# Group-norm sums from ScalarE's accumulator, and the order of ScalarE's, GpSimd's and TensorE's work around them

## The chip, the cores and the metric

One core of a Trainium2 chip. The metric is the device time of one execution in microseconds; below, "the median" is that of three runs. The engines are TensorE (PE, its weight loads PEld), VectorE (DVE), ScalarE (ACT), GpSimd (POOL) and SyncE (SP), which here issues the DMAs. A name with q (POOLq) is the engine's sequencer.

## What is computed

Eight batches of 548 tokens (36 image patches, embedded, and 512 text tokens) with 192 features pass one attention layer with three heads of 64, decay in place of a mask and a group norm over each head's outputs, and one FFN of 16 experts with a top-8 router. Cut to what matters here:

```
h = concat(image @ W.T + b, txt)                        # (8, 548, 192)
q, k, v = layernorm(h) @ Wq.T, ... @ Wk.T, ... @ Wv.T   # 3 heads of 64
weights = softmax(q @ k.T / 8 * decay)                  # per head
o = weights @ v
mean, var = o.mean(axis=(tokens, 64)), o.var(axis=(tokens, 64))   # per batch and head
y = (o - mean) / sqrt(var + 1e-5) * gn_weight + gn_bias
h = h + y @ Wo.T
x2 = layernorm(h)
h = h + sum over experts e of comb[:, e] * (gelu(x2 @ w1[:, e]) @ w2[e, :])
```

## The kernel before

All products are made in split precision: an operand is rounded to fp32r (hi), the rest is kept (lo), and PE adds hi x hi, lo x hi and hi x lo. ACT rounds (a Copy that writes hi), DVE subtracts (lo); POOL does both for w1 and w2.

**Attention** is a loop over the batches, written out by hand for each engine; `body(b, ...)` of an engine is its part of batch b together with what is left of batch t = b - 1. PE's order in it: q and k of batch b in three products of ten matmuls (`qk`, the third gives head 3's q in rows 0 to 63 and its k in rows 64 to 127), the transposes of the third head's weights of batch t (`probs_transpose(t, 2)`), the scores of heads 1 and 2 (`scores_pair`), `attend(t, 2)`, head 3's scores (`scores_third`), v (`values`), the output product of batch b - 2 (`project`), then transposes and `attend` for heads 1 and 2 of b, the transposes of the next batch's tokens (`x_transpose`) and the group-norm sums of t (`gn_sums`). A full first pass of qk needs xa and xb, which ACT rounds (`x_hi`) and DVE subtracts (`x_lo`), after DVE's sum over tokens (`x_ext`).

ACT's order in `body`: rounding q, k (`qk_round`), copying attention outputs from PSUM to `ot` (`o_copy`, two halves each), copying transposed weights to `pt` (`pt_copy`, four groups of a head), exps, v. PSUM has eight banks and each product has its fixed banks, so ACT's copies decide when PE may write again. Head 3's k is wanted in rows 0 to 63 also: ACT copies `k2_hi[HD:P]` to `k2_hi[0:HD]`, and `scores_third` waits for it (fifth count of `qk_hi`).

**The group norm of batch t.** DVE takes `bn_stats` of `ot` in `gn_stats`, for heads 1 and 2 early in `body` and for head 3 after `add_attention`, and `gn_partial` turns them into mean and mean of squares (`gmv`). PE multiplies `gmv` with `head_mean` (1/64 in each head's block), ACT reads the totals (`gn_totals`), POOL makes scale and shift (`gn_coefficients`, seven small steps with drains) and for batches 0 to 5 also y itself (`y_values`: two scalings, two casts, two subtractions). For the last two batches ACT makes y (`y_round`, `y_whole`) beside the FFN.

**The FFN** runs over nine slabs of tokens (`t`), 24 tiles of 128 hidden columns each (steps j, k = j within the slab). PE does `up(j + 3)` and `down(j)`, five matmuls each; ACT does `gelu(j + 1)` and `act_round(j)`, DVE the product with the gate (L1347) and the subtraction. `beside_first(k)` on each of these engines gives what else is done in step k of slab 0: the end of attention for batches 6 and 7 and the tokens of slab 1. `x2_transpose(1, 0)` is PE's at step 8, `x2_round(1, ...)` ACT's at 8 and 10, y of the last batch ACT's at 9 and 11. POOL's program behind the loop is short: coefficients of batch 6, then w2 in eight parts (`split_w2`, L658 to L662), with `second_rstd(1)`, `norm_second` (the scaling of slab 1's tokens, L584) and the last batch's coefficients between them. SP loads part p only when part p - 2 is split.

Of the kernel before, what the change touches and what calls it, by code (L numbers as in the profile page):

```python
# [32 lines left out]
P = 128  # L33
# [52 lines left out]
def width(t):  # L86
    return WIDTHS[t]
# [68 lines left out]
def early_fusion(nc, first_patches, patches, txt, tok_w, tok_b, gammas, gn_w, gn_b, attn_w, w1, w2, out):  # L156
# [9 lines left out]
    with ctx:  # L166
# [92 lines left out]
        gst, gmv, gtot = sb("gst", [P, 2, 12]), sb("gmv", [P, 2, 2]), sb("gtot", [P, 2, 2])  # L259
        gvar, grstd = sb("gvar", [P, 2]), sb("grstd", [P, 2])  # L260
        gscale, gshift, gtmp = sb("gscale", [P, 2]), sb("gshift", [P, 2]), sb("gtmp", [P, 2])
# [69 lines left out]
        def _(sp):  # L331
# [96 lines left out]
            def load_res(t):  # L428

                if t == 4:  # L430
                    sp.wait_ge(xn2_ready, 2)
                elif t >= 3:
                    sp.wait_ge(ln2_normed, max(t - 3, 1))
                r = width(t) // segs(t)
                sp.dma_start(res[t % 3][:r, 0:segs(t), :], by_segment(h_dram, t)).then_inc(ld_res[t % 3], 16)
# [94 lines left out]
        def _(pool):  # L530
# [19 lines left out]
            pool.memset(head_mean[0:HD, 0:HD], 1.0 / HD)  # L550
            pool.memset(head_mean[HD:P, HD:P], 1.0 / HD)
# [25 lines left out]

            def norm_second():

                r = width(1) // segs(1)  # L580
                pool.wait_ge(ld_res[1], 16)
                apart(pool, "pool")
                for g in range(SEG):
                    pool.tensor_scalar(xn2[:r, g, 0:D], res[1][:r, g, :], rstdb[:r, g:g + 1], nmrb[:r, g:g + 1], ALU.mult, ALU.add)  # L584
                pool.drain()
                pool.tensor_copy(xn2[:, :, D:256], xn2[:, :, P:D]).then_inc(xn2_ready, 1)
# [22 lines left out]
            def gn_coefficients(t):  # L609
# [15 lines left out]
                pool.tensor_tensor(gsub[:, :], gtot[:, :, 0], gscale[:, :], ALU.mult)  # L625
# [23 lines left out]
            def second_twice(t):  # L649
                twice(ln2_normed, 1, xn2, xn2_ready)  # L650
# [50 lines left out]
        def _(sc_eng):  # L701
# [104 lines left out]
            def o_copy(b, hh, bank):  # L806
# [5 lines left out]
                for half, n in enumerate(ATTEND_W):  # L812
                    p = HD * (hh % 2)
                    last = copy(ot[b % 2][p:p + HD, hh // 2, at:at + n], ps[HD * half:HD * half + HD, bank, 0:n])
                    at += n
                last.then_inc(o_copied, 1)

            def gn_totals(t, bank=GN_BANK):
# [3 lines left out]
                copy(gtot[:, :, :], ps[:, bank, GN_AT:GN_AT + 4].rearrange("p (i k) -> p i k", i=2)).then_inc(gn_read, 1)  # L822
# [38 lines left out]
            def body(b, tail, later, more, ahead):  # L861
# [72 lines left out]
            def beside_first(k):  # L934

                if k == 3:
                    y_round(LB - 1, 0)
                    y_whole(LB - 1, 0)
                elif k == 2:
                    o_copy(LB, 2, LAST_O[2])  # L940
                elif k == 4:
                    y_round(LB - 1, 1)
                    y_whole(LB - 1, 1)
                elif k == 6:
                    gn_totals(LB, LAST_GN[LB])
                elif k == 8:
# [45 lines left out]
        def _(dve):  # L992
# [23 lines left out]
            dve.memset(gmv[:, :, :], 0.0)  # L1016
# [871 lines left out]
```

## Time and profile before

| | |
|---|---|
| median of three runs | 757.18 us (756.56 to 757.28) |
| the profiled execution | 758.12 us |
| its span | 756.3 us |
| TensorE's mean granted clock | 0.992 of full speed |
| busy: PE, DVE, ACT, POOL | 719.2, 575.8, 469.2, 159.2 us |
| attention, batches 0 to 7 | about 16 to 240 us |
| FFN, slab 0 | about 243 to 310 us |
| FFN, slabs 1 to 8 | from 310 us to the end |

The profiled execution's time is that of the whole execution, the span runs from its first to its last instruction. Matmuls overlap, so a busy PE is not PE at its peak. An idle time is printed at the instruction that ended it, with what released it, in brackets. A line of the profile is a line of the kernel before; L705 is ACT's copy, L1462 PE's matmul and L1079 DVE's subtraction, all helpers, so that the names in a row tell which it is.

### The profile page before, as it was taken

The numbers are of one execution on the slowest core, as the hardware profiler recorded it, in microseconds if no ns is written. First come the engines' busy times: TensorE is split into PE (matmuls) and PEld (weight loads), VectorE is DVE, ScalarE is ACT, GpSimd is POOL, SyncE is SP. The second block draws the span as 40 slices with busy tenths as digits, with TensorE's granted clock in tenths as the row PEclk, the third lists the DMA queues.
The fourth block names the chain that finished last, engine by engine and source line by source line (L and its number), as shares of the span: only waits on it lengthen the run. The fifth ranks groups of instructions, "written<-read, shape, count | busy, mean of one in ns | idle before, by whom it ended". The sixth has DMA issues, their size and how long they took to land.

```text
span 756.3 us, 13059 instructions
## 1 busy us (share of the span) xinstructions
PE 719.2 (95%) x4205; PEld 601.1 (79%) x4205; DVE 575.8 (76%) x1591; ACT 469.2 (62%) x1049; POOL 159.2 (21%) x278
## 2 busy tenths in 40 slices
PE   6988999999999887999999999999999999999997
PEld 5777888889888666887887887887887887888896
DVE  7899888988887755777777777777777777777675
ACT  2678788778787826455655655655655655655653
POOL 3062564574551881000000000000000000000000
PEclk9999999999999998999999999999999999999999
DMA  6700011011112641443463453553553553551432
GB/s 197 212 23 4 21 44 44 3 44 47 63 44 65 192 133 34 102 110 95 96 152 93 95 156 91 109 141 91 117 140 84 123 140 79 112 156 46 100 84 54
DMA packets 124357, 70.57 MB, mean 93 GB/s; under 512 B 85792, under 2 KB 104288, under 8 KB 124288
## 3 DMA queue, kind: packets, MB, share of 16 engines
q1 hardware_dynamic: 124288, 69.74, 36.6%
q8 instruction: 33, 0.54, 0.3%
q14 instruction: 36, 0.29, 0.1%
HBM read 58.65 MB, written 10.63 MB: 92 GB/s over the span
## 4 chain that ended last, share of the span: by engine, by line
PE 74%; ACT 9%; DVE 7%; POOL 3%; issue 2%; POOLq 2%; SPq 2%; DMA 1%; DVEq 1%; ACTq 0%
PE ps L1462 72%; ACT pt L705 3%; ACT ot L705 2%; ACT pr L785 1%; DVE pr L1138 1%; PE ps L1611 1%; POOL w_lo L661 1%; ACT k_hi L705 1%; DVE sc L1116 1%; DMA pat<-patches 1%; POOL xn L584 1%; DVE xb L1079 1%; ACT xa_hi L705 1%; DVE xa_lo L1079 1%; POOL w_r L659 1%
## 5 line engine op out<-in xcount | busy, mean ns | idle before, releaser
L925 ACT ACTIVATE act<-ps 128x512 f32<-128x512 f32 (+1 forms) x216 | 124.6, 577 | 189.6 <-PE ps L1462 189.0
L1347 DVE TENSOR_TENSOR act<-act,gate 128x512 f32<-128x512 f32 (+1 forms) x216 | 146.1, 677 | 109.4 <-ACT act L925 89.5
L1462 PE MATMUL ps<-x,w_hi 128*128 128x512 f32 (+1 forms) x648 | 215.3, 388 | 6.8 <-ACT act L925 6.8
L1462 PE MATMUL ps<-x,w_lo 128*128 128x512 f32 (+1 forms) x432 | 165.7, 384 | 0.0
L1462 PEld LDWEIGHTS ps<-x,w_hi 128*128 128x128 f32 x648 | 121.0, 189 | 33.4 <-ACT act L925 8.2
L1079 DVE TENSOR_TENSOR act_lo<-act,act_hi 128x512 fp32r<-128x512 f32 (+1 forms) x216 | 144.2, 668 | 0.2
L705 ACT ACTIVATE act_hi<-act 128x512 fp32r<-128x512 f32 (+1 forms) x216 | 130.3, 603 | 5.4 <-DVE act L1347 5.2
L1462 PEld LDWEIGHTS ps<-x,w_lo 128*128 128x128 f32 x432 | 81.5, 189 | 16.7
L556 POOL TENSOR_TENSOR rstdb<-vepsb,neg_half 128x4 f32<-128x4 f32 x9 | 9.7, 1073 | 368.9 <-DVE vepsb L1202 368.9
L1462 PE MATMUL ps<-act_hi,w_hi 128*128 128x512 f32 (+1 forms) x216 | 83.5, 387 | 1.9 <-DVE act_lo L1079 1.7
L1462 PE MATMUL ps<-act_lo,w_hi 128*128 128x512 f32 (+1 forms) x216 | 83.2, 385 | 0.0
L1462 PE MATMUL ps<-act_hi,w_lo 128*128 128x512 f32 (+1 forms) x216 | 83.2, 385 | 0.0
L1462 PE MATMUL ps<-act_lo,w_r 128*128 128x512 f32 (+1 forms) x216 | 82.4, 382 | 0.0
L1462 PE MATMUL ps<-act_hi,w_r 128*128 128x512 f32 (+1 forms) x216 | 81.5, 377 | 0.0
L785 ACT ACTIVATE pr<-sc,nm 128x580 f32<-128x580 f32 (+4 forms) x120 | 66.3, 556 | 12.8 <-DVE nm L1123 12.8
L705 ACT ACTIVATE pt<-ps 128x384 f32<-128x384 f32 (+3 forms) x120 | 46.5, 472 | 12.1 <-PE ps L1611 11.8
L1611 PE MATMUL ps<-ident,pr 128*128 128x128 f32 (+1 forms) x360 | 44.3, 274 | 8.6 <-DVE q_lo L1079 3.2
L1116 DVE CUSTOM_DVE_ANT_0 sc<-ps,decay 128x548 f32<-128x548 f32 (+4 forms) x120 | 49.4, 453 | 3.8 <-PE ps L1462 3.8
L1462 PEld LDWEIGHTS ps<-act_hi,w_hi 128*128 128x128 f32 x216 | 40.7, 188 | 13.1 <-DVE act_lo L1079 4.5
L1611 PEld LDWEIGHTS ps<-ident,pr 128*128 128x128 f32 (+1 forms) x360 | 38.4, 132 | 13.1 <-issue 5.5
L1462 PEld LDWEIGHTS ps<-act_hi,w_r 128*128 128x128 f32 x216 | 40.6, 188 | 9.0
L1462 PEld LDWEIGHTS ps<-act_lo,w_r 128*128 128x128 f32 x216 | 40.4, 187 | 9.0
(187 smaller groups left out, 1198.1 us busy)
## 6 DMA issues: line engine op xcount, KB each, us to landing
gate<-comb_dram SPq DMA_DIRECT2D x128, 256.0 KB, 4.2
w_raw<-w SPq DMA_DIRECT2D x16, 384.0 KB, 3.7
h_dram<-h SPq DMA_DIRECT2D x8, 384.0 KB
res<-h_dram SPq DMA_DIRECT2D x8, 384.0 KB, 3.9
rb<-h_dram SPq DMA_DIRECT2D x48, 64.0 KB, 2.4
out<-rb SPq DMA_DIRECT2D x48, 64.0 KB, 1.9
x_dram<-xn_t SPq DMA_DIRECT2D x24, 96.0 KB, 2.4
gate<-comb_dram SPq DMA_DIRECT2D x16, 144.0 KB, 3.0
```

The lines of the kernel that those rows point to most:

```text
L556: pool.tensor_tensor(rs[:, :], ve[:, :], neg_half[:, 0:n], ALU.pow)
L584: pool.tensor_scalar(xn2[:r, g, 0:D], res[1][:r, g, :], rstdb[:r, g:g + 1], nmrb[:r, g:g + 1], ALU.mult, ALU.add)
L659: pool.tensor_copy(w2_r[:, part, :], raw[:, :, P:256])
L661: pool.tensor_tensor(w2_lo[:, part, :], raw[:, :, 0:P], w2_hi[:, part, :], ALU.subtract)
L705: return a.activation(dst, src, ACT.Copy)
L785: last = a.activation(pr[s][:r, cols], sc[s][:r, cols], ACT.Exp, bias=nm[s][:r, I:I + 1], accum_out=row_sum[s][:r, I:I + 1])
L925: a.activation(act[j % 3][:, 0:n], ps[:, up_bank(j), 0:n], ACT.Gelu_apprx_tanh).then_inc(gelu_done, 1)
L1079: return dve.tensor_tensor(dst, src, hi, ALU.subtract)
L1116: dve.tensor_tensor_reduce(out=sc[s][:r, OFF[I]:OFF[I] + n], in0=psf[:r, at:at + n], in1=decay[:r, hh, 0:n], scale=1.0 / 8, scalar=0.0 if ...
L1347: dve.tensor_tensor(act[j % 3][:, 0:n], act[j % 3][:, 0:n], gate[e % 4][:, 0:n], ALU.mult).then_inc(gated, 1)
L1462: return pe.matmul(dst, w, x, start=start, stop=stop)
L1611: return pe.transpose(ps[:n, bank, at:at + P], pr[s][:, src:src + n], ident[:, :])
```

## The change

Four parts. (1) The group norm's sums: each half of `o_copy` becomes an activation with `accum_out` into `gsums` (columns 0 and 1), a new `square` on ACT (Square over `ot`, with `accum_out` into column 2) gives the sum of squares, in rows of heads 1 and 2 (i = 0) and of head 3 (i = 1). DVE's `gn_stats` and `gn_partial` are gone, `head_mean` holds 1/(64 x 548), the product has six columns instead of four, and POOL adds the two halves' means first (`gmean`). (2) ACT's order: head 3's k behind the first two groups of `pt_copy(t, 2)`, head 3's `o_copy` and square ahead of `pt_copy(b, 0)`, and `x_hi(b + 1, 0)` ahead of `o_copy(b, 0)`. The copy of head 3's k to rows 0 to 63 goes from ACT to the end of DVE's `qk_rest`. PE's first group of `probs_transpose(t, 2)` no longer waits for q's lo part. (3) POOL behind the loop: `second_rstd(1)` behind part 1, `gn_coefficients(LB)` behind part 3. (4) `norm_second` is gone; ACT scales slab 1's tokens at steps 5 and 7, and POOL only duplicates 64 columns (`second_twice(1)`). Waits are adapted to that.

```diff
-                    last = copy(ot[b % 2][p:p + HD, hh // 2, at:at + n], ps[HD * half:HD * half + HD, bank, 0:n])
+                    last = a.activation(ot[b % 2][p:p + HD, hh // 2, at:at + n], ps[HD * half:HD * half + HD, bank, 0:n],
+                                        ACT.Copy, accum_out=gsums[b % 2][p:p + HD, hh // 2, half:half + 1])
...
+            def square(t, i):
+
+                r = Y_ROWS[i]
+                a.wait_ge(o_copied, nth(t, 3, i + 2))
+                last = a.activation(squares[:r, :], ot[t % 2][:r, i, :], ACT.Square, accum_out=gsums[t % 2][:r, i, 2:3])
+                if i:
+                    last.then_inc(gn_part, 1)
...
                 qk_round(b, 2)
+                if tail:
+                    pt_copy(t, 2, (0, 1))
                 qk_round(b, 3)
                 if tail:
-                    pt_copy(t, 2)
-                a.wait_ge(qk_hi, nth(b, 5, 4))
-                copy(k2_hi[0:HD, :], k2_hi[HD:P, :]).then_inc(qk_hi, 1)
+                    pt_copy(t, 2, (2, 3))
+                if tail:
+                    square(t, 0)
...
-                pt_copy(b, 0)
                 if tail:
                     o_copy(t, 2, O_BANKS[2])
+                    square(t, 1)
+                pt_copy(b, 0)
                 if more:
                     exps(b, 2, (0, 1))
                     pt_copy(b, 1)
+                    x_hi(b + 1, 0)
                     o_copy(b, 0, O_BANKS[0])
-                    x_hi(b + 1, 0)
                     x_hi(b + 1, 1)
...
+                elif k == 0:
+                    square(LB, 0)
                 elif k == 2:
                     o_copy(LB, 2, LAST_O[2])
+                    square(LB, 1)
...
+                elif k == 5:
+                    second_norm(1, 0)
+                elif k == 7:
+                    second_norm(1, 1)
...
+                dve.tensor_copy(k2_hi[0:HD, :], k2_hi[HD:P, :]).then_inc(qk_hi, 1)
...
-                if tail:
-                    gn_stats(t, 0)
...
-                if tail:
-                    gn_partial(t)
...
             split_w2(1)
+            second_rstd(1)
             split_w2(2)
-            second_rstd(1)
-            pool.drain()
-            pool.wait_ge(x2t_done, 2)
-            norm_second()
-            for p in range(3, W2_PARTS - 1):
+            split_w2(3)
+            second_twice(1)
+            gn_coefficients(LB)
+            for p in range(4, W2_PARTS):
                 split_w2(p)
-            gn_coefficients(LB)
-            split_w2(W2_PARTS - 1)
...
+                    probs_transpose(t, 2, (0,))
                     pe.wait_ge(qk_lo, nth(b, 4, 1))
-                    probs_transpose(t, 2, (0, 1, 2))
+                    probs_transpose(t, 2, (1, 2))
```

Three places show how the instructions stand. ACT, from the rounding of q to the first exp of head 1, in a batch of the loop (k_hi of 64 rows is head 3's k, `pt` the third head's weights of the batch before), before and then changed:

```order
L705 ACTIVATE q_hi<-ps 128x548
L705 ACTIVATE k_hi<-ps 128x548
L705 ACTIVATE ot<-ps 64x292
L705 ACTIVATE ot<-ps 64x256
L705 ACTIVATE q<-ps 64x548
L705 ACTIVATE k_hi<-ps 64x548
L705 ACTIVATE pt<-ps 68x2x256
L705 ACTIVATE pt<-ps 68x36
L705 ACTIVATE pt<-ps 128x384
L705 ACTIVATE pt<-ps 128x512
L705 ACTIVATE pt<-ps 128x384
L705 ACTIVATE k_hi<-k_hi 64x548
```

```order
L694 ACTIVATE q_hi<-ps 128x548
L694 ACTIVATE k_hi<-ps 128x548
L803 ACTIVATE ot,gsums<-ps 64x292
L803 ACTIVATE ot,gsums<-ps 64x256
L694 ACTIVATE q<-ps 64x548
L694 ACTIVATE pt<-ps 68x2x256
L694 ACTIVATE pt<-ps 68x36
L694 ACTIVATE pt<-ps 128x384
L694 ACTIVATE k_hi<-ps 64x548
L694 ACTIVATE pt<-ps 128x512
L694 ACTIVATE pt<-ps 128x384
L812 ACTIVATE squares,gsums<-ot 128x548
```

Head 3's k stands behind three of the five pt copies, its duplicate is gone, and a square stands in the duplicate's place.

ACT again, from the last exps of head 2 to those of head 3 of the same batch (`ot` is the output of head 3 of the batch before), before and then changed:

```order
L785 ACTIVATE pr,row_sum<-sc,nm 128x324
L785 ACTIVATE pr,row_sum<-sc,nm 128x196
L785 ACTIVATE pr,row_sum<-sc,nm 36x68
L705 ACTIVATE pt<-ps 68x2x256
L705 ACTIVATE pt<-ps 68x36
L705 ACTIVATE pt<-ps 128x384
L705 ACTIVATE pt<-ps 128x512
L705 ACTIVATE pt<-ps 128x384
L705 ACTIVATE ot<-ps 64x292
L705 ACTIVATE ot<-ps 64x256
L785 ACTIVATE pr,row_sum<-sc,nm 128x580
```

```order
L774 ACTIVATE pr,row_sum<-sc,nm 128x324
L774 ACTIVATE pr,row_sum<-sc,nm 128x196
L774 ACTIVATE pr,row_sum<-sc,nm 36x68
L803 ACTIVATE ot,gsums<-ps 64x292
L803 ACTIVATE ot,gsums<-ps 64x256
L812 ACTIVATE squares,gsums<-ot 64x548
L694 ACTIVATE pt<-ps 68x2x256
L694 ACTIVATE pt<-ps 68x36
L694 ACTIVATE pt<-ps 128x384
L694 ACTIVATE pt<-ps 128x512
L694 ACTIVATE pt<-ps 128x384
L774 ACTIVATE pr,row_sum<-sc,nm 128x580
```

The two halves of `ot`, now with sums, and a square stand ahead of the first head's pt copies.

POOL behind the loop, around the last batch's coefficients (w_hi, w_lo and w_r are w2's parts), before: the last rows of part 3 and on to part 4, where the change has the coefficients; then the change at the same place:

```order
L661 TENSOR_TENSOR w_lo<-w_raw,w_hi 128x384
L662 TENSOR_TENSOR w_r<-w_raw,w_r 128x3x64
L658 CAST w_hi<-w_raw 128x384
L659 CAST w_r<-w_raw 128x384
L661 TENSOR_TENSOR w_lo<-w_raw,w_hi 128x384
L662 TENSOR_TENSOR w_r<-w_raw,w_r 128x3x64
```

```order
L650 CAST w_r<-w_raw 128x384
L652 TENSOR_TENSOR w_lo<-w_raw,w_hi 128x384
L653 TENSOR_TENSOR w_r<-w_raw,w_r 128x3x64
L564 COPY xn<-xn 128x4x64
L604 TENSOR_TENSOR gmean<-gtot 128x2
L606 TENSOR_TENSOR gsquare<-gmean 128x2
L608 TENSOR_TENSOR gvar<-gtot,gsquare 128x2
```

Between the fourth and the fifth part (3 and 4) there stand now one copy and the eight steps of the coefficients, of which the first three rows are shown; before, the coefficients stood behind part 6.

## Rows read from the trace of the kernel before

**Rows 1.** Page, part 1: busy time, share, instructions.

```profile
PE 719.2 (95%) x4205; PEld 601.1 (79%) x4205; DVE 575.8 (76%) x1591; ACT 469.2 (62%) x1049; POOL 159.2 (21%) x278
```

**Rows 2.** Chain of waits, batch 5: start, us, what (PE only).

```profile
158.54 2.07 PE ps L1462 x14
...
164.61 11.71 PE ps L1462 x109
...
185.85 2.07 PE ps L1462 x14
```

**Rows 3.** Timeline, FFN: start, us, engine, instruction, idle before and releaser.

```profile
285.17 0.84 ACT L826 ACTIVATE y<-ot,gshift,gscale 128x548 fp32r<-128x548 f32 x1 [6.67 <-POOL gshift L627]
...
287.28 0.79 PE L1462 MATMUL ps<-x,w_hi 128*128 128x512 f32 x1 [5.92 <-ACT act L925]
```

**Rows 4.** Timeline of POOL, behind the loop.

```profile
256.57 0.96 POOL L658 CAST w_hi<-w_raw 128x384 fp32r<-128x384 f32 x1
...
262.87 6.24 POOL L584 TENSOR_SCALAR xn<-res,rstdb,nmrb 128x192 f32<-128x192 f32 x4 [0.32 <-issue]
...
282.33 0.20 POOL L615 TENSOR_TENSOR gsquare<-gtot 128x2 f32<-128x2 f32 x1
```

**Rows 5.** Busy time by stretch: PE, PEld, DVE, ACT, POOL; clock, DMA, GB/s.

```profile
285.00:290.00 5.00, 2.72 (x7) 2.13 (x8) 1.62 (x2) 2.58 (x4) 2.59 (x5) 0.50 0.12 30
```

**Rows 6.** Timeline of ACT, steps 8 and 9 of slab 0.

```profile
276.89 0.60 ACT L705 ACTIVATE x<-ps 128x512 fp32r<-128x512 f32 x1 [6.64 <-PE ps L1658]
...
277.87 0.63 ACT L705 ACTIVATE act_hi<-act 128x512 fp32r<-128x512 f32 x1
```

**Rows 7.** Timeline of PE, steps 8 to 10 of slab 0.

```profile
276.26 0.60 PE L1658 MATMUL ps<-ident,xn 128*128 128x128 f32 x4
...
278.04 0.51 PE L1462 MATMUL ps<-x,w_hi 128*128 128x512 f32 x1
...
289.58 1.06 PE L1658 MATMUL ps<-ident,xn 128*128 128x128 f32 x4
```

**Rows 8.** Groups by form: count, busy us, mean ns, idle before.

```profile
L705 ACT ACTIVATE act_hi<-act 128x512 fp32r<-128x512 f32 x192 | 119.8, 624 | 4.7 <-DVE act L1347 4.4
...
L785 ACT ACTIVATE pr<-sc,nm 128x580 f32<-128x580 f32 x24 | 18.6, 773 | 12.8 <-DVE nm L1123 12.8
L785 ACT ACTIVATION_READ_ACCUMULATOR pr<-sc,nm 128x1 f32 x96 | 18.4, 191 | 0.0
...
L1138 DVE TENSOR_SCALAR pr<-pr,inv_den 128x580 f32<-128x580 f32 x24 | 12.6, 526 | 2.2 <-issue 0.4
```

**Rows 9.** Timeline, batch 5: exps, subtraction of k, third decay, PE behind.

```profile
163.52 0.73 DVE L1079 TENSOR_TENSOR k_lo<-ps,k_hi 64x548 fp32r<-64x548 f32 x1
...
170.72 0.07 DVE L1116 DVE_READ_ACCUMULATOR2_ANT mx<- 36x1 f32 x1
...
171.24 0.27 PE L1462 MATMUL ps<-aw_hi,xa_hi 128*128 128x192 f32 x1
...
179.30 0.77 ACT L785 ACTIVATE pr<-sc,nm 128x580 f32<-128x580 f32 x1
...
180.06 0.20 ACT L782 ACTIVATE zero_score<-nm 128x5 f32<-128x5 f32 x1
```

**Rows 10.** Timeline of ACT, batch 5: pt copies, outputs, xb.

```profile
176.79 1.92 ACT L705 ACTIVATE pt<-ps 68x512 f32<-68x512 f32 x5 [1.30 <-PE ps L1611]
...
182.71 0.81 ACT L705 ACTIVATE ot<-ps 64x292 f32<-64x292 f32 x2
...
184.10 0.65 ACT L705 ACTIVATE xb<-ps 128x580 fp32r<-128x580 f32 x1
```

**Rows 11.** Timeline of POOL, batch 5: subtractions of y and w1.

```profile
164.43 1.37 POOL L643 TENSOR_TENSOR y<-ot,y 128x548 fp32r<-128x548 f32 x1 [0.17 <-issue]
...
180.40 1.96 POOL L603 TENSOR_TENSOR w_lo<-w_raw,w_hi 128x384 fp32r<-128x384 f32 x2
```

**Rows 12.** Tile gtmp: DVE's product, min/median/max ns, from and to.

```profile
L1155 DVE TENSOR_TENSOR gtmp<-gmv x8: 160/750/765, 71.4 to 262.3; 128x2 f32<-128x2 f32 x8
```

More of the change, by code:

```diff
@@ L258, in early_fusion @@
         inv_den = [sb(f"inv_den{i}", [P, NT]) for i in range(2)]
-        gst, gmv, gtot = sb("gst", [P, 2, 12]), sb("gmv", [P, 2, 2]), sb("gtot", [P, 2, 2])
+        gsums, gtot = [sb(f"gsums{i}", [P, 2, 3]) for i in range(2)], sb("gtot", [P, 2, 3])
+        squares, gmean = sb("squares", [P, L]), sb("gmean", [P, 2])
         gvar, grstd = sb("gvar", [P, 2]), sb("grstd", [P, 2])
-        gscale, gshift, gtmp = sb("gscale", [P, 2]), sb("gshift", [P, 2]), sb("gtmp", [P, 2])
+        gscale, gshift = sb("gscale", [P, 2]), sb("gshift", [P, 2])
         gsub, gsquare = sb("gsub", [P, 2]), sb("gsquare", [P, 2])
@@ L428, in load_res @@
             def load_res(t):
[L430 to L433, printed above, removed]
+                if t >= 3:
+                    sp.wait_ge(ln2_normed, t - 2)
                 r = width(t) // segs(t)
@@ L614, in gn_coefficients @@
                 apart(pool, "pool")
-                pool.tensor_tensor(gsquare[:, :], gtot[:, :, 0], gtot[:, :, 0], ALU.mult)
+                pool.tensor_tensor(gmean[:, :], gtot[:, :, 0], gtot[:, :, 1], ALU.add)
                 pool.drain()
-                pool.tensor_tensor(gvar[:, :], gtot[:, :, 1], gsquare[:, :], ALU.subtract)
+                pool.tensor_tensor(gsquare[:, :], gmean[:, :], gmean[:, :], ALU.mult)
+                pool.drain()
+                pool.tensor_tensor(gvar[:, :], gtot[:, :, 2], gsquare[:, :], ALU.subtract)
                 pool.drain()
@@ L624, in gn_coefficients @@
                 pool.drain()
-                pool.tensor_tensor(gsub[:, :], gtot[:, :, 0], gscale[:, :], ALU.mult)
+                pool.tensor_tensor(gsub[:, :], gmean[:, :], gscale[:, :], ALU.mult)
                 pool.drain()
@@ L649, in second_twice @@
             def second_twice(t):
-                twice(ln2_normed, 1, xn2, xn2_ready)
+                twice(ln2_normed, t + 1, xn2, xn2_ready)
             def split_w2(p):
@@ L821, in gn_totals @@
                     a.wait_ge(y_coeff, nth(t - 1, 1, 1))
-                copy(gtot[:, :, :], ps[:, bank, GN_AT:GN_AT + 4].rearrange("p (i k) -> p i k", i=2)).then_inc(gn_read, 1)
+                copy(gtot[:, :, :], ps[:, bank, GN_AT:GN_AT + 6].rearrange("p (i k) -> p i k", i=2)).then_inc(gn_read, 1)
             def y_of(dst, t, i):
@@ L1015, in _ @@
             dve.memset(comb[:, :, :], 0.0)
-            dve.memset(gmv[:, :, :], 0.0)
+            for t in (0, 1):
+                dve.memset(gsums[t][:, :, :], 0.0)
             dve.memset(k2_lo[HD:P, :].bitcast(F32), 0.0)
@@ L1139, in normalise @@
                 last.then_inc(probs_ready, 1)
-            def gn_stats(t, i):
-                dve.wait_ge(o_copied, nth(t, 3, i + 2))
-                for j in range(2):
-                    dve.bn_stats(gst[:Y_ROWS[i], i, 6 * j:6 * j + 6], ot[t % 2][:Y_ROWS[i], i, j * HALF:(j + 1) * HALF])
-            def gn_partial(t):
-                gn_stats(t, 1)
-                if t:
-                    dve.wait_ge(gn_sum, nth(t - 1, 1, 1))
-                dve.drain()
-                for i in range(2):
-                    dve.bn_aggr(gmv[:Y_ROWS[i], i, :], gst[:Y_ROWS[i], i, :])
-                dve.drain()
-                dve.tensor_tensor(gtmp[:, :], gmv[:, :, 0], gmv[:, :, 0], ALU.mult)
-                dve.drain()
-                dve.tensor_tensor(gmv[:, :, 1], gmv[:, :, 1], gtmp[:, :], ALU.add).then_inc(gn_part, 1)
             def y_rest(t, parts=(0, 1)):
@@ L1190, in second_part @@
                     dve.wait_ge(ld_res[t % 3], 16 * (t // 3 + 1))
[L1191 to L1194 removed]
+                    if t >= 2:
+                        dve.wait_ge(ln2_normed, t)
                 for g in ((0, 1), range(2, n), ())[part]:
@@ L1273, in turn_x2 @@
                 r = width(t) // n
-                dve.wait_ge(ln2_normed, t)
+                dve.wait_ge(ln2_normed, t + 1)
                 for g in (range(2), range(2, n))[half]:
```

24 lines of the change are left out of this document (4 added, 20 removed).

## Prediction

> **What bounds the kernel now.** I read the page first: TensorE (PE) is busy 95% of the 756.3 us span [rows 1]. Two stretches are not PE's own pace. In attention (about 16 to 240 us) the batches repeat every 27.3 us: the chain of waits of batch 5 runs from PE's xb pass at 158.54 to the next at 185.85, and in it PE alone works from 164.61 to 176.32; the rest is ScalarE's (ACT) copies and VectorE (DVE) [rows 2]. Seven batches (1 to 7) have this form. The other stretch is the first slab of the FFN. There PE stands still for 5.92 us until ACT gives it a gelu, ACT has waited 6.67 us for gshift, and GpSimd (POOL) begins the coefficients that end in gshift only at 282.33, after seven of w2's eight parts [rows 3, 4]. Behind it the granted clock is 0.50 in 285 to 290 us, the lower of the two levels, after PE had been idle [rows 5]. From 310 us on PE runs through to the end, and the change touches nothing there that PE waits for.
>
> **The FFN part.** POOL loses the four scalings of the second slab's tokens, 6.24 us from 262.87, which go to ACT as two pairs at steps 5 and 7 of the slab. The final coefficients go from behind part 6 to behind part 3. POOL's new order: parts 0 and 1 until 256.6 as before; second_rstd 2.0 (ends 258.6); part 2 in the 3.0 to 4.0 that it takes now between 256.57 and 260.6, part 3 likewise, to about 266; the duplicate copy, which waits for ACT's step 7; then the coefficients. ACT idles 6.64 us today, from 270.25 to 276.89, behind its round of step 8 [rows 6]. The added pairs, four activations of 192 columns at under 0.6 us each (an exp of 580 takes 0.773 [rows 8]), find room in the smaller gaps before that, so I put ln2_normed at 269.5 and the duplicate's end at 270.2; all four behind 270.25 would make it 273.1. The coefficients took from 282.33 to ACT's release at 285.17, 2.8 us [rows 3, 4], with the added mean 3.2: gshift is there at 273.4, at 276.3 at worst. ACT asks for it after its round of step 9, which began at 277.87 [rows 6], at 278.5. The margin is 5 us, 2 at worst, so the 6.67 us wait goes whole. The later parts of w2 then end at about 276, 279, 282.5 and 286, and the down passes want them from step 12 on, behind 284: the DMAs on SP's queue that wait for parts 4 and 5 come out within half a microsecond of now.
> PE then starts the up pass of step 10 at about 281.2 instead of 287.28: 6.1 gained. At the low clock the five up matmuls took 2.30 us (287.28 to 289.58) and four transposes 1.06; at the high one a first up matmul of 0.51 and four at 0.23 to 0.24 apart make 1.2 from 278.04, and four transposes took 0.60 [rows 3, 7]: 1.5 gained. Next late is act_lo of step 11, since ACT still runs its transposed-token copy and the y copies in that order; I put it at nothing gained and nothing lost. Against it stand 0.2 for the accumulator reads in the last o_copy before the first gelu. Squares at steps 0 and 2 lie in ACT's waits for DVE. DVE loses its group-norm statistics there and meets a POOL that splits without a pause; I let these cancel, cover being PE's queue of three up passes. **FFN: -6.1 - 1.5 + 0.2 = -7.4 us.**
>
> **One batch of attention.** Prices first. A plain ACT copy of 512 columns takes 0.624, an exp of 580 with accumulator 0.773, and the read behind it 0.191; yet the instruction behind exp and read starts 0.76 after the exp [rows 8, 9], so the read is all but hidden in the exp's own drain. It costs some 0.10 where two copies would have overlapped, and next to nothing behind o_copy, whose two halves (0.81 together [rows 10]) hardly do. No row has a Square or a Copy with accumulator. Bounds for a read: 0 and 0.19; I take 0.02. For a square of 548 columns: 0.55 (a copy's pace) to 0.77 (the exp); taken 0.65, nearest the copy. DVE's copy of 64x548: 0.46 (the scaling of pr, 0.526 for 580, less some overlap) to 0.73 (the subtraction from PSUM [rows 9]); taken 0.46, because like the scaling it has one source in SBUF.
> - **Scores.** k2's duplicate (0.66) leaves ACT, and k2's own copy (0.65) goes behind the first three pt copies. PE's scores start at 164.61 - 0.65 + 0.04 = 164.0. But k2_hi then ends at 164.36, DVE's k_lo at 165.12 (before 164.25 [rows 9]), the duplicate at 165.58, the norm statistics (1.3) at 166.9: the first decay starts 0.15 late, the 0.71 us of gst that left DVE notwithstanding. Its third one of head 1 ends at 170.95 instead of 170.80; PE took it up at 171.24 and would now be there at 170.6 [rows 9]. Gain 0.3, not 0.6. The first transposes of the third head no longer wait for q_lo; they would start 0.1 to 0.2 sooner, but the copies behind them wait for ACT, so that counts nothing.
> - **First head's pt.** The exps end 0.15 late, at 175.6. Now o_copy (0.86) and a square (0.65) come before the pt copies, where ACT idled 1.30 us [rows 10]. The copies start at 177.08 instead of 176.79; PE's attend and the second head's transposes slip 0.27. Behind them ACT is 0.4 early, since its o_copy is done.
> - **Next batch's x.** PE's x transposes slip 0.27 to 181.56. DVE is free there now (it ended its group-norm sums at 182.5), so the first reduce ends at about 182.98 and xa_hi starts at 183.0 instead of 183.55. But o_copy stands between xa_hi and xb: xb starts at 183.0 + 0.55 + 0.86 = 184.41, against 184.10 [rows 10]. DVE, which then had xa_lo to end first, finishes xb 0.06 to 0.15 later than now.
> Sum: +0.1 a batch, **+0.7 us for seven**. gn_sums, waiting for a sum that ACT made long before, costs PE nothing new.
>
> Total: 758.12 (the profiled execution, span 756.3) - 7.4 + 0.7 = 751.4. That execution lay 0.94 above the median of the runs, 757.18; against the median the forecast is **750.5 us**.
>
> **Where a rule speaks against it.** DVE multiplied two columns (gtmp) in 0.75 us in the median of the eight batches and in 0.16 at least [rows 12]; in batch 5 it ended together with the two subtractions of 0.98 us that POOL had begun at 180.40 [rows 11]. POOL runs L643, 1.37 us, from 164.43 [rows 11]; with the later gtot (0.25) and the added mean (0.35) it starts at 165.03, a tenth before DVE's new copy at 165.12. The Trainium skill (SBUF — State Buffer, Who interferes with whom) says that a DVE copy inside SBUF can take the ports that it shares with GpSimd, and that the later of two such instructions blocks until the earlier ends. By that rule the copy would take up to 1.3 us more; gtmp agrees, but no row here has a copy of this kind beside a subtraction.
> The square at its upper row, 0.77, would add 0.12 for each of the seven batches in the second step, 0.8 in all.
>
> **Rivals.**
> 1. *The copy blocks.* DVE copy behind L643, 1.3 us more. Slack there is 0.44, of which 0.15 is used; PE's 0.3 gain turns into a loss of 1.0, and all behind it shifts: +1.3 for each of the six batches in which POOL computes y: 750.5 + 7.8 = 758.3. For it: gtmp. Against it: a tenth decides who is first. Chance 0.18, and a partial block lies between.
> 2. *Slower: the reads count in full on ACT.* Place: o_copy and squares, five ACTIVATEs and their reads on the chain in the second and third steps above, two in front of the scores. Price: 0.19 each instead of 0.02 is 7 x 0.17 = 1.2, squares 0.74 instead of 0.65, so some +1.4 a batch, 7 x 1.4 = 9.8: 750.5 + 9.8 = 760.3. It decides from 1.2 us a batch on (8.2 / 7, to 758.7). For it: ACT's 1.30 us of slack is spent by o_copy and square alone. Against it: the exps show an overlapped read. Chance 0.10.
> 3. *A second stall behind the first.* In the FFN POOL or the pairs on ACT come late (the duplicate waits for step 7, PE's transposes at step 8 for it), or PE meets ACT's queue at steps 9 to 11, and half the gain stays away: 750.5 + 3.7 = 754.2. Chance 0.12.
> 4. *The loop gains.* The halves of o_copy overlap once the read stands between, or the reads cost nothing: -0.3 to -0.4 a batch in place of +0.1: 750.5 - 3.1 = 747.4. Chance 0.09.
> The forecast itself has 0.51, with 747.5 to 753.5 for its own prices.
>
> **The numbers.** Range 746.5 to 758: forecast, rivals 1 and 3 and most of 4; it leaves out rival 2, the upper half of rival 1 and tails, some 0.2. About 0.2% (1.5 us) is what a measurement of this kernel can tell from no change. Faster (below 755.7): forecast, 3, 4 and a partial rival 1: 0.77. Same: most of rival 1, 0.12. Slower (above 758.7): rival 2 and a full block with dearer reads, 0.11.
>
> **What the profile will show.** Right: no ACT wait for gshift and no PE gap above 1 us between 250 and 300; no clock of 0.5 there; batches 27.2 to 27.6 apart; scores start less than 5.6 us behind the xb pass (6.07 before), but the first decay hardly moves; ACT has no idle before the first head's pt copies. Wrong: batches over 28 apart, with a DVE k2 copy above 1 us (rival 1) or reads with 0.19 between starts (rival 2); a PE gap above 2 us at step 8 or 10 (rival 3); below 27.0 apart (rival 4).

## The result, and the profile after

| | before | changed |
|---|---|---|
| median, 4 runs each | 757.23 us (756.56 to 757.45) | 762.87 us (761.74 to 763.02) |
| the profiled execution's span | 756.3 us | 761.2 us |
| batch 5, from one xb pass to the next | 27.3 us | 29.2 us |

The ratio is 1.0074 with a 95% interval of 1.0063 to 1.0086: 5.6 us slower, where 6.7 us faster was forecast. The changed profile, part 1 of the page:

```profile
PE 719.5 (95%) x4205; PEld 599.6 (79%) x4205; DVE 565.3 (74%) x1536; ACT 482.4 (63%) x1125; POOL 158.6 (21%) x282
```

Against [rows 1], ACT has 13.2 us and 76 instructions more (the reads of the accumulators are instructions), DVE 10.5 us and 55 fewer. PE has the same work, so what grew is its waiting. What PE waits for, by releaser, in the changed kernel (total us, times, longest):

```profile
PE ps L1444 <- ACT pt L694: 6.5, 12, 1.2
PE ps L1444 <- DVE mx L1126: 6.3, 7, 1.5
...
PE ps L1444 <- DVE act_lo L1088: 4.1, 5, 1.9
PE ps L1444 <- DVE xb L1088: 3.0, 8, 0.5
```

The second row is the new one: matmuls of attention that wait for the decay's maxima, 1.2 to 1.5 us in each of batches 2, 3, 5 and 6, and 0.25 in batches 1 and 4 (the seventh is 0.19). The reason for this split comes below.

**The difference of the spans, cut in four.** I take the ends of DVE's subtractions of xb, one a batch, and the first gelu. Up to batch 0's xb: 20.91 us before, 21.31 now, +0.4. Seven batches: 192.16 and 201.29, **+9.1**. From the last xb to the first gelu: 34.57 and 35.28, +0.7. From there to the end: 508.66 and 503.32, **-5.3**. The sum is +4.9, which is the difference of the spans. So the FFN part did what it should and the loop lost far more than the +0.7 forecast.

**The FFN.** ACT's y behind step 9 and the first down pass that waits behind it, in the timelines of ACT and PE (start, us, instruction, idle before and releaser):

```profile
289.04 0.85 ACT L824 ACTIVATE y<-ot,gshift,gscale 128x548 fp32r<-128x548 f32 x1
```

```profile
290.92 0.50 PE L1444 MATMUL ps<-act_hi,w_hi 128*128 128x512 f32 x1 [0.80 <-DVE act_lo L1088]
...
298.47 0.50 PE L1444 MATMUL ps<-act_hi,w_hi 128*128 128x512 f32 x1 [1.91 <-DVE act_lo L1088]
```

There is no wait for gshift (6.67 us in [rows 3]) and no gap of 5.92 us on PE; what is late next is act_lo, 0.80 and 1.91 us. The clock is up at this place, as a stretch of the table by windows shows (its columns are those of [rows 5], where the clock was 0.50):

```profile
285.00:290.00 5.00, 4.99 (x23) 3.51 (x21) 1.83 (x3) 2.46 (x5) 4.71 (x8) 1.00 0.26 76
```

It is not up everywhere: where attention passes into the FFN, both kernels run 3.4 us at a granted clock of 0.50 (from 239.5 us before, from 250.0 us changed). The kernel before has a second such stretch, of 6.8 us from 283.9, which begins within the 5.92 us that PE waits; the changed one has not.

**The loop.** DVE's new copy of head 3's k, all eight of them (min, median and max ns, first and last start):

```profile
L1116 DVE CAST k_hi<-k_hi x8: 433/1610/1639, 26.8 to 229.4; 64x548 fp32r<-64x548 f32 x8
```

Its price has two values. In batches 0, 1 and 4 it takes 0.43 us, in the other five 1.60 us and more. In batches 0 and 1 POOL runs nothing beside it. In the six others POOL runs its subtraction of y at that moment, and batch 4 is the only one of them that escapes. DVE and POOL in batch 3, then in batch 4:

```profile
114.17 1.62 DVE L1116 CAST k_hi<-k_hi 64x548 fp32r<-64x548 f32 x1
...
143.34 0.43 DVE L1116 CAST k_hi<-k_hi 64x548 fp32r<-64x548 f32 x1
```

```profile
114.12 1.38 POOL L634 TENSOR_TENSOR y<-ot,y 128x548 fp32r<-128x548 f32 x1 [0.17 <-issue]
...
143.46 1.56 POOL L634 TENSOR_TENSOR y<-ot,y 128x548 fp32r<-128x548 f32 x1 [0.17 <-issue]
```

In batch 3 POOL began 0.05 us before the copy, and the copy ended 0.29 behind POOL's end at 115.50. In batch 4 the copy began 0.12 before, kept its 0.43, and POOL's subtraction took 1.56 instead of 1.38. Batch 4 is 28.07 us long, batches 3 and 5 are 29.17: the held copy costs **1.10 us** of a batch. But batch 4, where nothing is held, is still 0.8 us longer than before. ACT at the end of batch 4:

```profile
161.59 0.65 ACT L694 ACTIVATE xa_hi<-ps 128x580 fp32r<-128x580 f32 x1 [0.56 <-DVE ps L1097]
162.15 0.39 ACT L803 ACTIVATE ot<-ps 64x292 f32<-64x292 f32 x1
162.44 0.19 ACT L803 ACTIVATION_READ_ACCUMULATOR ot<-ps 64x1 f32 x1
162.64 0.38 ACT L803 ACTIVATE ot<-ps 64x256 f32<-64x256 f32 x1
162.93 0.19 ACT L803 ACTIVATION_READ_ACCUMULATOR ot<-ps 64x1 f32 x1
163.14 0.66 ACT L694 ACTIVATE xb<-ps 128x580 fp32r<-128x580 f32 x1
```

From the first half's start to xb's start there are 0.99 us; before, from the same o_copy's start to the next copy's, there were 0.84 (182.71 to 183.55). The half at 162.15 starts 0.10 before the end of xa in front of it, and a read starts 0.10 before the end of its half in the same way; but what follows such a read starts only when the read is done. In front of the first head's pt copies (ACT, the same batch):

```profile
153.73 0.19 ACT L774 ACTIVATION_READ_ACCUMULATOR pr<-sc,nm 36x1 f32 x1
153.82 0.40 ACT L803 ACTIVATE ot<-ps 64x292 f32<-64x292 f32 x1
154.12 0.20 ACT L803 ACTIVATION_READ_ACCUMULATOR ot<-ps 64x1 f32 x1
154.33 0.38 ACT L803 ACTIVATE ot<-ps 64x256 f32<-64x256 f32 x1
154.61 0.19 ACT L803 ACTIVATION_READ_ACCUMULATOR ot<-ps 64x1 f32 x1
154.83 0.66 ACT L812 ACTIVATE squares<-ot 64x548 f32<-64x548 f32 x1
155.40 0.19 ACT L812 ACTIVATION_READ_ACCUMULATOR squares<-ot 64x1 f32 x1
155.61 1.92 ACT L694 ACTIVATE pt<-ps 68x512 f32<-68x512 f32 x5
```

o_copy and square take 1.79 us where ACT once idled 1.30 [rows 10]; the sum had 0.86 + 0.65 = 1.51 for them. From this o_copy's start to the next instruction's there are 1.01 us, where the kernel before had 0.72 (178.58 to 179.30); but there an exp followed, here a square, so the 0.29 between them is not the price of two reads. Run 6 below has plain halves in front of the same square, and takes 0.83. From the square's start to the pt copies' there are 0.78 us, its read included.

Behind the exps a read acts otherwise: at 153.73 the last exp's read (0.19 us) begins, and the o_copy starts at 153.82, 0.10 before its end. That is so behind 93 of the 120 reads of exps, and behind none of the 48 of o_copy.

### The profile page after: what moved, and what is told of

It is laid out like the page before. It is cut to its first block, busy times and chain, and to the rows that moved or that the text cites. A ratio compares the mean times of both kernels' runs of the same rounds, so it can differ in the third digit from the quotient of the medians.

```text
span 761.2 us, 13065 instructions
## 1 busy us (share of the span) xinstructions
PE 719.5 (95%) x4205; PEld 599.6 (79%) x4205; DVE 565.3 (74%) x1536; ACT 482.4 (63%) x1125; POOL 158.6 (21%) x282
## 4 chain that ended last, share of the span: by engine, by line
PE 67%; ACT 14%; DVE 10%; issue 3%; DMA 2%; SPq 2%; DVEq 1%; POOL 1%; POOLq 1%
PE ps L1444 65%; ACT pr L774 5%; ACT ot L803 3%; ACT pt L694 2%; DVE sc L1126 2%; PE ps L1593 2%; ACT k_hi L694 1%; DMA gate<-comb_dram 1%; DVE k_hi L1116 1%; ACT v L694 1%; DVE st L1042 1%; DVE k_lo L1088 1%; DMA pat<-patches 1%; DVE ps L1097 1%; DVE xb L1088 1%
## 5 line engine op out<-in xcount | busy, mean ns | idle before, releaser
L1444 PEld LDWEIGHTS ps<-x,w_hi 128*128 128x128 f32 x648 | 120.9, 189 | 27.2 <-ACT act L926 2.0
L1444 PE MATMUL ps<-pt,v 128*64 128x128 f32 (+3 forms) x432 | 43.9, 345 | 3.5 <-ACT pt L694 3.5
```

Of the source, the lines that this page charges most:

```text
L1444: return pe.matmul(dst, w, x, start=start, stop=stop)
```

## The experiments

Theory: three separate costs in the loop, the held copy, the reads and head 3's square. Rivals: the copy does not matter, or the reads do not, or the two halves of the change depend on each other. The numbers are the labels'. In all below, "a batch" is batch 5, from one xb end to the next: 27.31 us before, 29.17 in the changed kernel. Behind a median stand, in brackets, its ratio to the kernel before, which ran beside it, and the 95% interval of that ratio; the kernel before was at 757.1 or 757.2 (756.8 beside run 12). A run has 4 to 10 executions, of which one is profiled.

**1, 2. Each half of the change alone.** The first is the kernel before with the parts (3) and (4), the second the changed kernel without them:

```diff
             split_w2(1)
-            split_w2(2)
             second_rstd(1)
-            pool.drain()
-            pool.wait_ge(x2t_done, 2)
-            norm_second()
-            for p in range(3, W2_PARTS - 1):
-                split_w2(p)
+            split_w2(2)
+            split_w2(3)
+            second_twice(1)
             gn_coefficients(LB)
-            split_w2(W2_PARTS - 1)
+            for p in range(4, W2_PARTS):
+                split_w2(p)
...
```

> The kernel before with the FFN part of the change alone: w2's parts, second_rstd and the last coefficients in the new order on POOL, slab 1's tokens scaled on ACT at steps 5 and 7. Theory (the two parts add up; the changed kernel's trace shows the loop +9.5 to +10.2 us and the first slab -5.3): 750 to 752 us, no PE gap over 1 us behind 250 us, batches still 27.3 apart. Rival (the two parts are not independent; the FFN part gains only because attention ended later and left POOL and DVE idle): above 753.5.

> The changed kernel with the FFN part undone: POOL's old order and its own scaling of slab 1's tokens. Theory (parts add up): 757.2 + 9.5 to 10.5 = 766.5 to 768.5, the wait of ACT for gshift is back with 5 to 7 us. Rival (the attention part's loss is smaller by itself): below 765.

Measured: 752.13 us (0.9927, 0.990 to 0.9954) with batches of 27.32, and 767.39 (1.0131, 1.0101 to 1.0162) with batches of 29.14. The two add up: -5.1 and +10.2 make +5.1, against +5.6 for both. In the second ACT's wait for gshift is back, in its timeline:

```profile
294.14 0.84 ACT L838 ACTIVATE y<-ot,gshift,gscale 128x548 fp32r<-128x548 f32 x1 [6.42 <-POOL gshift L630]
```

**3. The duplicate back on ACT.**

```diff
-                dve.tensor_copy(k2_hi[0:HD, :], k2_hi[HD:P, :]).then_inc(qk_hi, 1)
...
                     pt_copy(t, 2, (2, 3))
+                a.wait_ge(qk_hi, nth(b, 5, 4))
+                copy(k2_hi[0:HD, :], k2_hi[HD:P, :]).then_inc(qk_hi, 1)
                 if tail:
                     square(t, 0)
```

> The changed kernel with the duplicate of head 3's k back on ACT, behind the last pt copies and ahead of the square; nothing else moved. Theory (DVE's SBUF copy is held up while POOL's subtraction of y runs: 1.6 us in five batches, 0.43 in two; and 0.36 on DVE's path even where it is not held up): no batch above 28.3, all alike within 0.1 from batch 3 on, the first decay 8.2 to 8.4 us behind xb's end (8.7 to 9.9 in the changed kernel), total 762.9 - 3.3 - 0.3 x 7 = 757.5, from 756.5 to 759.6. Rival (the copy's length does not matter, ScalarE's accumulator reads are the whole loss): 762 or more, batches over 28.8.

Measured: 754.87 us (0.9972, 0.9956 to 0.9987), all batches but the first 27.7 (27.3 the last), the first decay 8.33 behind xb. That is 8.0 less than the changed kernel by one moved copy (6.7 between the two profiled executions), and below my range. The un-held copy costs 0.38 of a batch on DVE (28.07 to 27.69), as I had put down; but I had counted three held batches, 3.3 us, where the changed kernel has four before its last xb pass, and 4 x 1.10 is 4.4.

**4. DVE's copy earlier.**

```diff
                     dve.wait_ge(qk_hi, nth(b, 5, made))
+                    if made == 4:
+                        dve.tensor_copy(k2_hi[0:HD, :], k2_hi[HD:P, :]).then_inc(qk_hi, 1)
                     src = ps[p0:p0 + lo.shape[0], QK_BANKS[i]:QK_BANKS[i] + 2, 0:HALF]
                     sub(two(lo), src, two(hi)).then_inc(qk_lo, 1)
-                dve.tensor_copy(k2_hi[0:HD, :], k2_hi[HD:P, :]).then_inc(qk_hi, 1)
```

> The changed kernel with DVE's duplicate of head 3's k ahead of the subtraction of k's lo part instead of behind it, so that it starts 0.65 us earlier, beside POOL's casts of y and before its subtraction. Theory (a copy that has begun before the subtraction is not held up, and casts do not hold it): copy 0.43 in every batch, batches 27.9 to 28.3 apart, total 762.9 - 3.3 = 759.6, from 759 to 760.5. Rival (POOL's casts hold the copy as well): copy 0.8 to 1.5 us, batches over 28.5, total 761.5 or more.

Measured: 760.15 us (1.0031, 1.0014 to 1.0049), batches 28.3 from batch 2 on. The time is the theory's, but its reason was half wrong. The copy of batch 2 on DVE, and what POOL ran there:

```profile
86.54 0.70 DVE L1115 CAST k_hi<-k_hi 64x548 fp32r<-64x548 f32 x1 [0.87 <-ACT k_hi L694]
```

```profile
85.52 1.42 POOL L631 CAST y<-ot 128x548 fp32r<-128x548 f32 x2
```

POOL's casts end at 86.94, the copy at 87.24, again 0.30 behind. A cast holds the copy as a subtraction does; only its rest was short. So it is in all six batches with casts: 0.70 to 0.73 us, against 0.44 in batches 0 and 1.

Batch 1 of this trace does not fit: 30.41 us, where the changed kernel has 28.10. The table by windows shows a possible reason, first the changed kernel, then this one:

```profile
70.00:75.00 5.00, 4.67 (x45) 4.15 (x47) 1.91 (x6) 4.56 (x13) 3.87 (x7) 1.00 0.00 0
```

```profile
70.00:75.00 5.00, 4.70 (x25) 3.74 (x26) 1.36 (x5) 2.91 (x9) 3.82 (x7) 0.51 0.00 0
```

The granted clock was 0.50, the lower of its two levels, from 68.1 to 74.9 us. PE had just waited 0.74 and 0.82 us (up to 66.3 and 67.7), but so it had in the changed kernel, where the clock stayed up. The traces of runs 11 and 5 have the same 6.8 us there, and batches 1 of 30.58 and 29.92; the kernel before, the changed one and runs 1 and 3 do not have it. That the clock made these batches long is read from where it stands, not tested, and no run shows why it fell. The batches from 2 to 6, on which the readings here rest, are at the full clock; how much of the loss the medians of runs 4, 5 and 11 contain is not known (run 11's ten executions range from 756.8 to 764.6 us).

**11. The duplicate read from PSUM.**

```diff
-                    sub(two(lo), src, two(hi)).then_inc(qk_lo, 1)
-                dve.tensor_copy(k2_hi[0:HD, :], k2_hi[HD:P, :]).then_inc(qk_hi, 1)
+                    last = sub(two(lo), src, two(hi))
+                    if made < 4:
+                        last.then_inc(qk_lo, 1)
+                dve.tensor_copy(two(k2_hi[0:HD, :]), src).then_inc(qk_lo, 1)
+                dve.sem_inc(qk_hi, 1)
```

> The changed kernel with DVE's duplicate of head 3's k rounded anew from PSUM instead of copied inside SBUF; PE's wait for the fourth lo part comes with it, 0.7 us later than now. Theory (only DVE's SBUF-to-SBUF copy is held while a POOL instruction runs, a read from PSUM is not): the duplicate takes 0.70 to 0.76 in every batch and starts beside POOL's subtraction in most; batches alike within 0.1, 28.3 to 28.6, total 760 to 761.5. Rival (any DVE instruction there is held): 1.4 to 1.9 us in four batches or more, total 762.5 or more.

Measured: 760.73 us (1.0052, 1.0028 to 1.0075), batches 28.2 from batch 2 on, but for one of 28.4. The copies by their line:

```profile
L1118 DVE CAST k_hi<-ps x8: 722/723/725, 26.9 to 229.4; 64x548 fp32r<-64x548 f32 x8
```

Eight times 0.72, at the same place in the batch: in batch 2 POOL's subtraction begins at 88.18 and this copy at 88.25, in the order that made it 1.60 us in the changed kernel. So what is held is the copy whose source and target both lie in SBUF. The Trainium skill (SBUF — State Buffer, Who interferes with whom) says just this: a copy in SBUF can run in a mode that takes the ports shared with GpSimd, whoever issues first has them for the whole instruction, and a DVE instruction with at most one input in SBUF outside those modes does not contend. These three runs agree, with 1.6 or 0.43, 0.70 and 0.72 us.

**6, 7. Reads and squares.** Both from run 3's kernel. Run 6 has o_copy with plain copies and leaves out the sums; run 7 has squares over one column and leaves out the other 547.

```diff
-                    last = a.activation(ot[b % 2][p:p + HD, hh // 2, at:at + n], ps[HD * half:HD * half + HD, bank, 0:n],
-                                        ACT.Copy, accum_out=gsums[b % 2][p:p + HD, hh // 2, half:half + 1])
+                    last = a.activation(ot[b % 2][p:p + HD, hh // 2, at:at + n], ps[HD * half:HD * half + HD, bank, 0:n], ACT.Copy)
```
```diff
-                last = a.activation(squares[:r, :], ot[t % 2][:r, i, :], ACT.Square, accum_out=gsums[t % 2][:r, i, 2:3])
+                last = a.activation(squares[:r, 0:1], ot[t % 2][:r, i, 0:1], ACT.Square, accum_out=gsums[t % 2][:r, i, 2:3])
```

> The same kernel (duplicate on ACT, 27.7 us a batch) with o_copy as two plain copies: the sums of the outputs are left out, so the group norm's mean is wrong; squares stay. Theory (each read costs 0.09 that two plain halves would have overlapped, 0.17 an o_copy, with two of the three o_copies on the path, head 3's ahead of the pt copies and head 1's between xa and xb): batches 27.35 to 27.45, total 752.7 to 753.3. Rival (the reads lie beside other waits and cost nothing): 754.5 or more.

> The same kernel (duplicate on ACT) with both squares on one column instead of 548: the sums of squares are left out, and the variance is wrong. Theory (head 3's square of 0.77 us stands on the path ahead of the first head's pt copies, with 0.4 beyond the idle time that ACT had there before; head 1 and 2's square stands in ACT's wait for the first decay and costs nothing): batches 27.3, total 752.1, from 751.5 to 753. Rival (squares lie in idle time altogether): 754.5 or more. Rival (both squares on the path): below 750.5.

Measured: 751.20 us (0.9911, 0.988 to 0.9942) and 750.71 (0.9912, 0.9887 to 0.9936). Without the six reads of its o_copies a batch is 26.87, **0.82** less, twice what I expected: the first decay comes 0.31 sooner (8.02 against 8.33), the reduce of the next tokens 0.64, xb on ACT 0.82, so each of the three o_copies gives some 0.2 to 0.3 on the path. From an o_copy's start to the next instruction's, run 3 has 1.12, 1.01 and 1.00 us (heads 2, 3 and 1), run 6 in the same places 0.82, 0.83 and 0.81: two reads take 0.30, 0.18 and 0.19 of ACT. With squares on one column a batch is 27.24, **0.45** less, as expected; the first decay keeps its place (8.34), so heads 1 and 2's square does lie in ACT's wait. The median of run 7 is 0.8 below its range. Up to the last xb its trace is 2.5 us shorter than run 3's, and from there to the first gelu another 1.9; there run 3's clock was 0.50 from 242.9 to 246.3, and run 7's stayed at 1.00. How much of the 1.9 is the clock's and how much the squares', no run separates.

**5, 8. xa and xb both ahead of o_copy.** In run 3's kernel, as below, and in run 1's, where o_copy stood ahead of both:

```diff
                     x_hi(b + 1, 0)
-                    o_copy(b, 0, O_BANKS[0])
                     x_hi(b + 1, 1)
+                    o_copy(b, 0, O_BANKS[0])
```

> The kernel with the duplicate of head 3's k back on ACT (27.7 us a batch, 754.9), with both roundings of the next batch's tokens (xa, xb) ahead of head 1's o_copy, where one was behind it. Theory (o_copy with its reads, 0.98, stands between xa and xb and delays DVE's xb and PE's second pass by the 0.37 us that PE waits there; the rest of the 0.98 is covered by PE's own attend): batches 27.3, total 752.3, from 751.5 to 753.3, PE's wait for xb under 0.1. Rival (all of the 0.98 is on the path, PE moves up with it): batches 26.9, total 749.5. Rival (the order makes no difference): 754 or more.

> The kernel before with the FFN part (752.1 us, 27.3 us a batch) and both roundings of the next batch's tokens ahead of head 1's o_copy; statistics on DVE, ACT's other order and the duplicate as before. Theory (ACT's order there is worth what PE waits for xb, 0.27): batches 27.0 to 27.1, total 750.3, from 749.8 to 751.3. Rival (DVE's group-norm sums ahead of x_ext hold the path, so the order gives nothing): 751.8 or more.

Measured: 753.50 us (0.9949, 0.9925 to 0.9973), batches 27.42, the median just above its range; and 754.58 (0.9968, 0.9954 to 0.9982), batches 27.46. The latter is 2.4 us slower than run 1, of which the seven batches are 1.0 in the traces; so the rival's "751.8 or more" holds, but not its reason: the order does not give nothing, it loses. PE's first pass over the next tokens in run 8 and in run 5:

```profile
186.91 0.52 PE L1450 MATMUL ps<-xa_hi,aw_hi 128*128 128x274 f32 x2 [0.68 <-ACT ot L691]
```

```profile
132.84 0.53 PE L1445 MATMUL ps<-xa_hi,aw_hi 128*128 128x274 f32 x2 [0.35 <-ACT ot L803]
```

q's banks include the one that o_copy has to empty first. With o_copy behind xb, PE's first pass waits for it; in run 8 that is more than the 0.27 that was to be had. With the reads in it, o_copy behind xb is still better than between xa and xb (27.42 against 27.69). Where o_copy is plain and short, the place between them was not tried by itself.

**9, 10, 12. The new order, with the sums left on DVE.** Run 1's kernel with ACT's and PE's order of the change, plain copies, no squares. Run 10 leaves DVE as before; run 9 puts its statistics where the changed kernel's DVE idles:

```diff
+                    if made == 4 and tail:
+                        gn_stats(b - 1, 0)
                     dve.wait_ge(qk_hi, nth(b, 5, made))
...
-                if tail:
-                    gn_stats(t, 0)
...
-                    gn_partial(t)
+                    gn_partial(t, (0,) if more else (0, 1))
                 if more:
                     x_ext(b + 1)
-                    x_lo(b + 1)
+                    x_lo(b + 1, (0,))
+                    if tail:
+                        gn_partial(t, (1,))
+                    x_lo(b + 1, (1,))
```

> The FFN part (752.1 us) with the change's order on ACT and PE (head 3's k behind three pt copies, head 3's o_copy ahead of the first head's pt copies, xa ahead of head 1's o_copy, xb behind it), but plain copies, no squares, the duplicate on ACT, and the group norm's sums on DVE, put where the changed kernel's DVE idles: bn_stats of heads 1 and 2 in its wait for k (0.87 us), of head 3 behind add_attention (1.7 us idle), the product and sum between xa_lo and xb (0.6 us idle). Theory (the loop's loss was reads 0.8 us and square 0.4 us a batch and the held copy; the new order itself gives 0.4 or more): batches 26.7 to 27.0, total 752.1 - 7 x 0.4 = 749.3, from 747.5 to 750.3. Rival (the order gives nothing without the sums on ACT, because DVE's statistics fill the same places): batches 27.2 or more, total 751.5 or more.

> As the run beside it, but DVE's statistics at their old places (behind k's lo part, and all of gn_partial ahead of the reduces of the next tokens). Theory (k's late rounding pushes bn_stats and with it the first decay to 8.7 or 8.8 us behind xb, and gn_partial holds the reduces as before): batches 27.3 to 27.6, total 752 to 753.5. Rival (the places on DVE do not matter): same as the run beside it, within 0.5.

Measured: 752.80 us (0.9939, 0.9921 to 0.9956) with a batch of 26.95, and 756.79 (0.9995, 0.9984 to 1.0007) with 28.15. The places on DVE are worth 1.2 us a batch; with the old ones the new order only loses (28.15 against run 1's 27.32, and my forecast was 27.3 to 27.6). Run 9's late batches are as forecast, its median is not (749.3): the first four batches are 27.2 to 28.5. In its end of a batch PE, and then ACT, wait for DVE's product and sum:

```profile
131.68 0.39 PE L1460 MATMUL ps<-gmv,head_mean 128*128 128x4 f32 x2 [0.30 <-DVE gmv L1146]
```

```profile
132.10 0.17 ACT L691 ACTIVATE gtot<-ps 128x4 f32<-128x4 f32 x1 [0.21 <-PE ps L1460]
```

Run 12 does them ahead of xa_lo:

```diff
                     x_ext(b + 1)
-                    x_lo(b + 1, (0,))
                     if tail:
                         gn_partial(t, (1,))
-                    x_lo(b + 1, (1,))
+                    x_lo(b + 1)
```

> The kernel with sums on DVE and the new order (26.94 us in its late batches, 752.8), with DVE's product and sum (0.31 us) ahead of xa_lo instead of between xa_lo and xb, since PE waits 0.30 us for them there. Theory (xb, ready at 132.70 where PE takes it up at 132.78, sets the second pass either way): PE's wait for gmv under 0.1, but batches 26.85 to 26.95, total 752.2, from 751 to 753. Rival (PE's 0.30 us is all on the path): batches 26.6 to 26.7, total 750.7 or less.

Measured: **747.85 us** (0.9888, 0.9868 to 0.9908), batches 26.59. The rival was right. I had followed PE alone, to xb. The same wait also held ACT's read of the totals, which stands ahead of the last three exps; behind those are DVE's scaling, its subtractions of q and k and the first decay. That decay now comes 8.08 us behind xb, 8.41 in run 9:

```profile
130.44 0.17 ACT L691 ACTIVATE gtot<-ps 128x4 f32<-128x4 f32 x1
```

Run 12 is the fastest kernel here, 9 us under the one before and 15 under the change. Not all of its 5 us on run 9 is this wait: between the two traces the seven batches give 2.1, and the stretch from the last xb to the first gelu 1.2.

## Why the prediction was wrong

It gave 750.5 us; 762.87 was measured, outside its range. The step that failed is the batch of attention, put at +0.1 us: the read at 0.02 and the copy at 0.46 were both too cheap. From the 751.4 forecast for the profiled execution to its 763.0, 8.4 us are the loop's, 2.1 the FFN's, and 1.1 lie before the first xb and between the last one and the first gelu. Step by step:

- **FFN, -7.4.** Right in mechanism, short in size. ACT rounds once a step of slab 0; in the changed kernel that stands 9.70 us later than before at step 0, 11.14 at step 8, 3.86 at step 10 and 4.44 at step 14. So the stall itself gave 7.3 us, against the forecast's 6.1 and 1.5. The "nothing lost" around it was not nothing: 1.4 us went ahead of it, and 0.6 behind. Run 1, without squares and reads, loses 0.5 ahead of it, so some 0.9 of the 1.4 goes with them; this is read from the two traces, not tested. By the cut of the spans the FFN gave 5.3, and run 1 alone gives 5.1 in the medians. Two signs were wrong with it: PE has a gap of 1.91 us between 250 and 300, and the clock was 0.50 from 250.0 to 253.5.
- **The read at 0.02.** The step that failed first. It was taken from the exps, where the instruction behind exp and read starts 0.76 after the exp. Behind those reads the next instruction starts 0.10 before the read ends; behind an o_copy's or head 3's square's it starts up to 0.03 after. So what the exps' rows hide is not hidden here. Run 6 measured 0.82 us a batch for six reads, 0.14 each, against the 0.12 that six times 0.02 would have made. Rival 2 had this, at 0.19 each.
- **Scores: "the first decay hardly moves".** It starts 8.26 us behind xb in batch 3 before, 8.69 in batch 4 changed, where the copy is not held, and 9.87 in batch 3, where it is. The forecast had 0.15 of this. In run 6, without the reads of head 2's o_copy in front of the third k, it came 0.31 sooner than in run 3, which is about what is left of the un-held case. The held copy is the rest of the other.
- **o_copy and square ahead of the pt copies.** Forecast as a shift of 0.27 with a square of 0.65; the square takes 0.78 with its read. Run 7, which takes all but one column out of it, is 0.45 a batch shorter.
- **The copy at 0.46.** Right where nothing held it (0.43), and held in five of eight batches (1.60 to 1.64). Rival 1 had the mechanism and nearly the price, 1.3 a held batch, where 1.10 was measured, but I gave it 0.18 on a tenth of a microsecond, and I let it hold in all six batches or in none, where it held in five.
- **The order's gain.** Of batch 5's +1.86 us, the runs account for 1.10 (held copy), 0.38 (copy on DVE at all), 0.82 (reads) and 0.45 (square), together 2.75. What is left, the new order and the statistics gone from DVE, is worth -0.89. On this sum the forecast's +0.1 came from prices set too low, not from gains that failed to come. The order alone is no gain: with the statistics at their old places it costs 0.83 (run 10 against run 1). The sum takes runs 6 and 7 as additive; leaving out both at once was not tried.
- **Rivals as alternatives.** Rivals 1 and 2 were priced at 758.3 and 760.3 as if one excluded the other. They came together, neither at its full price, which would have made 768.1. The case "both" had no chance of its own, and the upper end of the range stood below it.

What stays open: why batches 0 to 2 are longer than the later ones in several of these kernels, also where the clock is full (27.81 and 28.04 for batches 0 and 2 before); why the clock fell in batch 1 of runs 4, 5 and 11; and how much of the 1.6 us by which the traces differ before the first xb is chance.

## What to carry to other kernels

Before a copy inside SBUF moves to VectorE, look at what GpSimd runs at that moment: if it is a cast or a subtraction as here, count the rest of that instruction, or read the source from PSUM, where there is a copy of it. An activation with a sum costs its read on ScalarE's chain even where the trace draws the two as overlapping; compare the start-to-start distances of neighbours, with and without the read, for the very instruction and its follower. And when two rivals act at different places, give their sum a chance too.

## What the runs showed of the hardware

- Which of the two waits is set by a twentieth of a microsecond: with POOL 0.05 ahead, DVE's copy took 1.62 us instead of 0.43; with DVE 0.12 ahead, POOL's subtraction took 1.56 instead of 1.38. So batches of one kernel, with the same program, were 28.07 and 29.17 us long.
- A held copy ended 0.29 and 0.30 us behind the POOL instruction that held it, in the two cases read above, whether that was a subtraction or a cast.
- Six reads of 0.19 us were worth 0.14 us each on the path, though five of the six are drawn 0.10 inside their activation. What follows them starts 0.20 to 0.22 behind the read's start; what follows an exp's read starts 0.09 behind it.
